# Linear attention joined to wide attention, key sums in column halves, fp32 output projection

## The reference

```python
x = x + _L1_attn_ref(_layernorm(x), W_K, W_Q, W_V, W_O)      # wide attention: 16 heads of 128
x = x + _L1_xattn_ref(_layernorm(x), ctx, ctx, mask, ...)    # linear attention
x = x + _L1_ffn_ref(_layernorm(x), ...)                      # mix of 32 experts
...
# _L1_xattn_ref, 16 heads of 16, 64 features a head
q, k, v = heads(query, Wq, bq), heads(key, Wk, bk), heads(value, Wv, bv)
q_prime = relu(einsum('bhnd,fd->bhnf', q, Wqf))
k_prime = relu(einsum('bhnd,fd->bhnf', k, Wkf)) * attention_mask[:, None, :, None]
kv    = einsum('bhnf,bhne->bhfe', k_prime, v)
qkv   = einsum('bhmf,bhfe->bhme', q_prime, kv)
k_sum = sum(k_prime, axis=2)
qk_sum = einsum('bhmf,bhf->bhm', q_prime, k_sum)[..., None]
out = qkv / (qk_sum + 1e-08)
return out.transpose(0, 2, 1, 3).reshape(B, Sq, H) @ Wo.T + bo
```

## Time and profile before

| | us |
|---|---|
| median of 3 runs | 1010.68 |
| lowest, highest | 1008.80, 1012.94 |
| the profiled execution | 1011.92 |
| its span, first to last instruction | 1010.10 |

### The profile page before, as it was taken

The page is one execution under the profiler, slowest core; times in us unless marked ns, Lnnn a source line. Parts: engine busy times, 40 slices in busy tenths (PEclk is TensorE's granted clock), DMA queues, the critical chain, the costliest instruction groups (busy, mean ns, idle before and its releaser), DMA issues. The chain is left out here.

```text
span 1010.1 us, 19622 instructions
## 1 busy us (share of the span) xinstructions
PE 959.6 (95%) x7403; PEld 820.1 (81%) x7403; DVE 636.9 (63%) x1399; ACT 482.0 (48%) x1611; POOL 239.3 (24%) x257
## 2 busy tenths in 40 slices
PE   7999999999999999999999999999999888999877
PEld 5777777898788888888888888888888757777757
DVE  5678887897765666544554645464554555777854
ACT  3887877334455454353434534444444343344421
POOL 3455786760011111111111111111111130110000
PEclk9999999999999999999999999999999997899979
DMA  8000000003400000000000000000000070000002
GB/s 303 27 2 2 2 2 1 2 15 133 177 14 1 1 1 1 2 1 1 1 1 1 1 1 16 28 1 1 1 2 1 1 268 1 2 1 2 2 1 84
DMA packets 10395, 27.85 MB, mean 28 GB/s; under 512 B 1792, under 2 KB 6944, under 8 KB 9664
## 3 DMA queue, kind: packets, MB, share of 16 engines
q1 hardware_dynamic: 9584, 26.41, 7.2%
q10 hardware_dynamic: 720, 0.20, 0.1%
HBM read 24.51 MB, written 2.10 MB: 26 GB/s over the span
## 5 line engine op out<-in xcount | busy, mean ns | idle before, releaser
L938 POOL TENSOR_TENSOR wa_prob<-wa_prob,wa_rsum 128x512 f32<-128x512 f32 x64 | 67.5, 1055 | 412.5 <-DVE wa_rsum L1493 412.5
L1296 ACT ACTIVATE wa_prob<-wa_prob,wa_negmax 128x128 f32<-128x128 f32 x256 | 99.8, 391 | 56.8 <-DVE wa_negmax L1482 56.6
L41 PE MATMUL bank<-norm_xT_hi,wide_hi 128*128 128x512 f32 x256 | 106.0, 414 | 0.2 <-DVE norm_xT_lo L175 0.2
L42 PE MATMUL bank<-norm_xT_lo,wide_hi 128*128 128x512 f32 x256 | 101.0, 395 | 0.0
L43 PE MATMUL bank<-norm_xT_hi,wide_lo 128*128 128x512 f32 x256 | 101.0, 395 | 0.0
L1549 DVE TENSOR_TENSOR wa_z_lo<-bank,wa_z_hi 128x512 fp32r<-128x512 f32 x64 | 44.3, 691 | 86.6 <-ACT wa_z_hi L1330 86.2
L562 ACT ACTIVATE v_prob<-bank,la_negmax 128x128 f32<-128x128 f32 x256 | 91.1, 399 | 1.1 <-DVE la_negmax L640 1.1
L1304 ACT COPY wa_q<-bank 128x512 f32<-128x512 f32 x64 | 37.5, 586 | 99.0 <-PE bank L43 99.0
L1311 ACT COPY wa_v<-bank 128x512 f32<-128x512 f32 x64 | 37.3, 585 | 97.1 <-PE bank L43 97.1
L308 POOL TENSOR_TENSOR v_prob<-v_prob,la_rsum 128x512 f32<-128x512 f32 x64 | 66.5, 1041 | 52.5 <-DVE la_rsum L645 52.4
L41 PE MATMUL bank<-wide_hi,wa_z_hi 128*128 128x256 f32 x256 | 73.6, 287 | 1.7 <-DVE wa_z_lo L1549 1.4
(11 more groups left out here) (282 smaller groups left out, 2462.8 us busy)
## 6 DMA issues: line engine op xcount, KB each, us to landing
wide_raw<-in_wide_w SPq DMA_DIRECT2D x16, 512.0 KB, 6.4
em_w<-in_em_w SPq DMA_DIRECT2D x1, 4096.0 KB, 16.1
x<-in_x SPq DMA_DIRECT2D x4, 512.0 KB, 4.8
lc_kt<-in_ctx_rev SPq DMA_DIRECT2D x1, 2048.0 KB, 10.6
lc_toep<-in_toeplitz SPq DMA_DIRECT2D x1, 2048.0 KB, 14.5
out_x<-x SPq DMA_DIRECT2D x8, 256.0 KB, 2.9
li_kt<-in_ctx_rev SPq DMA_DIRECT2D x1, 1536.0 KB, 8.2
w_or_y<-in_l_w SPq DMA_DIRECT2D x1, 1024.0 KB, 6.5
```

Of the source, the lines that this page charges most:

```text
L41: nc.tensor.matmul(out, a[0], b[0], start=start, stop=False, skip_group_check=True)
L42: nc.tensor.matmul(out, a[0], b[1], start=False, stop=False, skip_group_check=True)
L938: nc.gpsimd.tensor_tensor(prob[:, s], prob[:, s], rsum[:, s, :].unsqueeze(2).to_broadcast([P, G, P]), ALU.mult).then_inc(prob_ok, 1)
L1296: last = nc.scalar.activation(prob[:, s, j, :], prob[:, s, j, :], ACT.Exp, bias=negmax[:, s, j:j + 1], scale=SCALE, accum_out=sums[:, s, j ...
```

## The change

- The barrier, the release of semaphores and the warm-up multiply are gone. Both stages become one, `stage_both_layers`: each engine goes on from the last head of wide attention into linear attention. Semaphores whose counts have ended are used again from the count that they reached (`Event`, `reached`).
- Buffers of linear attention lie over weights of wide attention that are no longer read (`layer.close()`). SyncE loads the constants before group 3, ctx in four pieces after head 4 of the last group, and the mix's weights after head 16.
- In the last group's heads, ACT, DVE and GpSimd get early work: the split of all of ctx in heads 6 to 9, the split of the weights Q, K, V in heads 10 to 12, norm statistics of images 4 to 7 in head 7 and their apply in head 14, three clears in head 10. TensorE runs the queries of images 0 to 3 behind the weighing of head 14, and the keys around that of head 15. The relu of the second query features is shared out between ACT (two banks) and DVE (two banks), in four banks of their own.
- Key sums: each head has its own matmul, 64 columns of weights and 32 moving columns, with results in partitions 0 to 63 and 64 to 127 (L1017), 16 matmuls in place of 8.
- The output projection is two plain fp32 matmuls of `o` and the unsplit weights (L1041) in place of six fp32r ones; the split of o is gone, `o` has two buffers.
- `vector_setup` moves from image 3 to image 1, the scaling in it (L2244) becomes `vector_length` in image 5, and the transposes of `em_simT` move from the tail into image 14. The wide weights' casts wait for all four pieces of a quarter.

```diff
--- stage_both_layers (was stage_attention_conv_experts_and_wide_attention)
+        layer.close()
+        mix = ExpertMix(pr)
+        linear = linear_attention(pr, lambda n, shape, dt=F32: ctx.enter_context(nc.sbuf_tensor(n, shape, dt)), mix)
+        mix.allocate(ctx)
...
+            linear.sync(sp)
+            mix.sync_stores(sp)
...
+                    if last and t == H - 1:
+                        linear.tensor_keys(pe, 0)
                     weigh(it, t)
+                    if last:
+                        linear.tensor_early(pe, t)
+                        norm.enter_stage(2, 1, b_p)
+                    if last and t == H - 1:
+                        linear.tensor_keys(pe, 1)
...
+            linear.tensor(pe)
+            mix.tensor_program(pe)
...
--- linear_attention
+    FIRST_BANKS = (banks[0], banks[1], banks[6], banks[7])
+    KT_AT, W_AT = 6, 10
+    QUERIES_AT, KEYS_AT = 14, 15
+    STATS_AT, CLEAR_AT, APPLY_AT = 7, 10, 14
     MIX_AT = {0: 3 * G, 1: 3 * G + 1, 2: 3 * G + 3}
+    SIM_AT = 3 * G + 2
+    SETUP_AT, LENGTH_AT = 1, 5
...
-        sp.dma_start(kt32[:, :, 0:G], io["ctx_rev"][:, :, 0:G]).then_inc(kt_first, 16)
+        sp.wait_ge(pr.wide_u_ps, 2 * (NG - 1))
         for t, src in ((bqk[:], io["li_bqk"]), (wf[:], io["li_wf"]), (mask[:], io["li_mask"]),
                        (v_bias[:], io["li_v_bias"]), (out_bias[:], io["li_o_bias"])):
-            sp.dma_start(t, src).then_inc(loaded, 16)
-        sp.wait_ge(kt_first, 16)
-        sp.dma_start(kt32[:, :, G:NB], io["ctx_rev"][:, :, G:NB]).then_inc(kt_loaded, 16)
+            sp.dma_start(t, src).then_inc(loaded.sem, 16)
+        heads_done(sp, 4)
+        for t in range(NG):
+            own = slice(t * G, (t + 1) * G)
+            sp.dma_start(kt32[:, :, own], io["ctx_rev"][:, :, own]).then_inc(kt_in.sem, 16)
+        heads_done(sp, H)
         mix.sync_loads(sp)
-        sp.dma_start(mix.w[:], io["em_w"]).then_inc(mix.w_loaded, 16)
+        sp.dma_start(mix.w[:], io["em_w"]).then_inc(mix.w_loaded.sem, 16)
...
+    def tensor_early(pe, t):
+        if t == QUERIES_AT:
+            norm.enter_stage(4, 2, [b_p] * 2)
+            pe.wait_ge(norm.s_lo, DC * norm.split(0))
+            reached(pe, w_lo, 3)
+            for m in range(DC):
+                queries(pe, 0, m, banks[m])
+
+    def tensor_keys(pe, m):
+        reached(pe, qT_ok, m + 1)
+        keys(pe, 0, m, banks[m])
...
         def key_values(n):
-            pe.wait_ge(kf_ok, n + 1)
-            pe.wait_ge(v_ok, n + 1)
+            reached(pe, kf_ok, n + 1)
+            reached(pe, v_ok, n + 1)
             wait(pe, kv_ok, n)
             wait(pe, x_ok, n - 1)
             for t in range(T):
-                last = nc.tensor.matmul(b_kv[:, t * 2 * VW:(t + 1) * 2 * VW], kp[:, n % 2, t, :],
-                                        va[:, n % 2, 2 * t:2 * t + 2, :], start=True, stop=True)
-            last.then_inc(kv_ps, 1)
+                for e in range(2):
+                    last = nc.tensor.matmul(b_kv[F * e:F * e + F, t * VW:(t + 1) * VW],
+                                            kp[:, n % 2, t, F * e:F * e + F], va[:, n % 2, 2 * t + e, :],
+                                            start=True, stop=True)
+            last.then_inc(kv_ps.sem, 1)
...
         def project(n):
-            pe.wait_ge(ot_lo, n + 1)
-            pe.wait_ge(kv_ok, min(n + 2, NB))
+            reached(pe, o_ok, n + 1)
+            reached(pe, kv_ok, min(n + 2, NB))
             wait(pe, x_ok, n)
             for c in range(DC):
-                last = product(nc, b_kv[:, 0:D], pair(oT, slice(None), n % 2, c), pair(w, slice(None), O, c),
-                               c == 0, c == DC - 1)
-            last.then_inc(o_ps, 1)
+                last = nc.tensor.matmul(b_kv[:, 0:D], o[:, n % 2, c, :], w32[:, O, c, :], start=(c == 0),
+                                        stop=(c == DC - 1))
+            last.then_inc(o_ps.sem, 1)
...
-        pe.wait_ge(pr.w_loaded, 16)
-        warm = w32.rearrange("p w c n -> p (w c n)")
-        for m in range(3):
-            nc.tensor.matmul(b_f[:, m, :], warm[:, m * P:(m + 1) * P], warm[:, 0:512], start=True, stop=True)
-        pe.wait_ge(w_lo, 1)
-        queries(0, 0, b_p)
-        queries(0, 1, b_nd)
-        pe.wait_ge(loaded, 16 * NLOAD)
+        reached(pe, loaded, 16 * NLOAD)
         query_features(0, 0)
-        pe.wait_ge(w_lo, 2)
-        keys(0, 0, b_p)
-        pe.wait_ge(qT_ok, DC)
-        keys(0, 1, b_nd)
-        pe.wait_ge(w_lo, 4)
+        first_query_features()
+        key_features(0)
+        reached(pe, qf_first, 1)
         values(0)
-        key_features(0)
+        turn_x(1, 0)
+        reached(pe, qf_ok, DC)
+        reached(pe, clear, 3)
+        key_values(0)
         values(1)
-        query_features(0, 1)
-        key_values(0)
...
+    def scalar_early(act, t):
+        if KT_AT <= t < KT_AT + NG:
+            own = slice((t - KT_AT) * G, (t - KT_AT + 1) * G)
+            reached(act, kt_in, 16 * NG)
+            nc.scalar.copy(kt[0][:, :, own], kt32[:, :, own]).then_inc(kt_hi.sem, 1)
+        if W_AT <= t < W_AT + 3:
+            n = (Q, K, V)[t - W_AT]
+            act.wait_ge(pr.w_loaded, 16)
+            heads_done(act, 8)
+            nc.scalar.copy(w[0][:, n], w32[:, n]).then_inc(w_hi.sem, 1)
+        if t == QUERIES_AT:
+            reached(act, loaded, 16 * NLOAD)
+            for m in range(DC):
+                keep_qT(act, 0, m, banks[m])
+        if t == KEYS_AT:
+            for m in range(DC):
+                keep_kT(act, 0, m, banks[m])
...
-        def keep_o(n):
-            act.wait_ge(o_ok, n + 1)
-            wait(act, o_ps, n - 1)
-            nc.scalar.copy(oT[0][:, n % 2], o[:]).then_inc(ot_hi, 1)
...
-        def o_rest(n):
-            dve.wait_ge(ot_hi, n + 1)
-            nc.vector.tensor_tensor(oT[1][:, n % 2], o[:], oT[0][:, n % 2].bitcast(F32), ALU.subtract)\
-                .then_inc(ot_lo, 1)
...
-            if n == 3:
+            if n == SETUP_AT:
                 mix.vector_setup(dve)
+            if n == LENGTH_AT:
+                mix.vector_length(dve)
```

More of the change, by code:

```diff
@@ L1 @@
+from collections import namedtuple
 from contextlib import ExitStack
@@ L21, with reached, __init__ @@
 BASE = 2
+Event = namedtuple("Event", "sem base")
+def reached(eng, event, count):
+    eng.wait_ge(event.sem, event.base + count)
 class Chain:
-    def __init__(self, eng, sem, it, per):
-        self.eng, self.sem, self.it, self.per, self.n = eng, sem, it, per, 0
+    def __init__(self, eng, sem, it, per, base=0):
+        self.eng, self.sem, self.it, self.per, self.n, self.base = eng, sem, it, per, 0, base
     def done(self, ins):
@@ L32, in done @@
         ins.then_inc(self.sem, 1)
-        self.eng.wait_ge(self.sem, self.it * self.per + self.n)
+        self.eng.wait_ge(self.sem, self.base + self.it * self.per + self.n)
     def close(self):
@@ L53, in __init__, with event @@
         self.sems = []
+        self.finished = []
+    def event(self, name):
+        return self.finished.pop(0) if self.finished else Event(self.sem(name), 0)
     def sem(self, name):
@@ L795, in stage_attention_conv_experts_and_wide_attention, with stage_both_layers @@
+def stage_both_layers(pr, layer, lora):
     nc, io, x, banks = pr.nc, pr.io, pr.x, pr.banks
@@ L966, in _ @@
                 group(it, it == NG - 1)
+            linear.gpsimd(pool)
+            mix.gpsimd_finish(pool)
         @block.tensor
@@ L1332, in group @@
                         high_part(FRONT_PIECES + t - 1)
+                    if last:
+                        linear.scalar_early(act, t)
                     for unit in late:
@@ L1385, in _ @@
                 group(it, it == NG - 1)
+            linear.scalar(act)
+            mix.scalar_program(act)
         @block.vector
@@ L1556, in group @@
                         low_part(FRONT_PIECES + t - 1)
+                    if last:
+                        linear.vector_early(dve, t)
                     if t == H - 1 and not last:
@@ L1628, in _, with both_layers @@
                 group(it, it == NG - 1)
-def first_layer_and_wide_attention(pr):
+            linear.vector(dve)
+            mix.vector_program(dve)
+def both_layers(pr):
     nc = pr.nc
@@ L2480, in stage_linear_attention_and_expert_mix @@
[L2480 to L2510 removed]
+        stage_both_layers(pr, ctx, lora)
```

1448 lines of the change are left out of this document (727 added, 721 removed).

## The result

The changed kernel takes 977.14 us (median of 4 runs, 976.68 to 977.83), the kernel before beside it 1011.71 (4 runs); the ratio is 0.9663 with a 95% interval of 0.9639 to 0.9686. Forecast were 978, and 967 to 993. The profiled execution took 976.68 us with a span of 974.90.

A forecast was written before the change was run, and what follows sets the result against it. TensorE was taken as the bound, busy 959.6 of 1010.1 us. Stretches A to H summed to 33.0 less, from the profiled 1011.92 to 978.9; 1.2 less for the median gave 977.7, so 978, range 967 to 993.

The forecast's parts named there:

- A: Junction up to nd(0), the start of numerators_and_denominators(0): 9.8 us less, nd(0) at 820.2 against 830.06.
- B: Stretch nd(0) to nd(1), image 0 to image 1: 13.00 to 5.1 us, 7.9 less.
- C: Stretch nd(1) to nd(2): 10.28 to 7.8 us, 2.5 less, half of it the clock.
- D: Stretch nd(2) to nd(4): 1.0 us less (0.5 to 1.5).
- E: Stretch nd(4) to nd(6): 21.01 to 15.0 us, 6.0 less, with L2244 no longer ahead of image 3's key features.
- The term for each image: Each image of the loop: 0.8 us less of TensorE, key sums 0.9 less and the fp32 projection 0.1 more.
- F: Stretch nd(6) to nd(12), 45.65 us before: 6 x 0.8 less 0.3, 4.5 us less.
- G: Stretch nd(12) to nd(15): 1.2 us less, as DVE sets the pace and loses three oT_lo of 0.42.
- H: From nd(15) on: 0.1 us less, split of o (0.9) gone, two fp32 projections 0.4 more each at the lower clock.
- Rival 4: Tail from nd(15) on: the clock stays up there, 970 us; chance 8%.
- Rival 1: Key sums: half-wide records run one after the other without overlap, no gain, costing 14: 992 us; chance 12%.
- Rivals 2, 3 and 5: Lower clock comes back, 986, 15%; narrow key-sum records cost as much as wide, 1021, 3%; early work doesn't hide, 993, 2%.

The follow-up runs named there:

- The late first work: Changed kernel with queries and keys of images 0 to 3 behind the last wide projection instead of in heads 14 and 15: 981.89 us.

## Why the prediction held, point by point

**A was right in size and in its reason.** nd(0) at 820.10 against 820.2, TensorE's wide work ending at 811.4 against 811.3, the wait for the x update 0.53 against 0.4. The late first work confirms 3.1 us of it. As said above, part of the agreement to 0.1 is luck, since single traces differ by up to 2 us before these heads. **The cover in the heads was not complete.** I costed the early work at 0, with head 7 at 6.9 of 7.84 us busy on DVE. But a busy share under 1 does not say that the order fits. The cast, the statistics and then the usual work of the changed kernel, behind each other on DVE, and the wait on TensorE:

```profile
752.33 1.22 DVE L1225 TENSOR_TENSOR li_kt_lo<-li_kt,li_kt_hi 128x1024 fp32r<-128x1024 f32 x1 [0.26 <-ACT li_kt_hi L1143]
753.48 1.40 DVE L126 BATCH_NORM_STATS2 norm_stats<-x 128x6 f32<-128x256 f32 x4
...
757.53 0.68 DVE L2461 COPY wa_probT<-bank 128x512 f32<-128x512 f32 x1
...
758.27 1.16 PE L2035 MATMUL bank<-wa_probT,wa_v 128*128 128x128 f32 x8 [0.60 <-DVE wa_probT L2461]
```

wa_probT comes late and weighing waits 0.60; the head lasts 8.60 instead of 7.85, the next 7.95. With the casts in the loop the same heads last 7.84 and 7.85. So the casts in the heads bring 0.6 in image 0 and cost 0.85 here.

**B was right in size, with the wrong share for the casts.** I named the chain and the casts together. The chunk of x before the loop is what matters: 5.5 of it (4.6 and 0.9). The casts alone are 0.6. The split of o, which the prediction held to be off the path in the middle of the loop, is worth 1.0 at its start: with it back nd(0) to nd(1) takes 6.45. **C and D** followed.

**E was right in size, and half wrong in its reason.** "In image 3 a 2.88 us DVE operation stands ahead of the key features" was true, but its move is worth 1.0 alone. With the casts and the split of o gone it is not needed for more, and with the split of o alone gone the wait falls from 1.79 to 1.34. The key sums in halves give 1.3 of the 5.84 (nd(4) to nd(6) takes 16.50 with the wide ones). The clock adds to the waits: outside the tail those of 1.34, 1.42, 1.44 and 1.45 us, and one of 1.65 at 243 us in every trace, left it up; those of 1.79, 1.99, 2.13, 2.14, 2.99 and 3.76 were followed by the lower level.

**The term for each image was too large**: 0.8 forecast, 0.49 measured (F). Three sizes make it up. Key sums gave 0.77 of the 0.9 (0.90 from first to last record, but the last takes 0.15 until the next step begins). The projection cost 0.15, the upper end of its bounds, where 0.1 was taken. And the step from the values to the key sums takes 0.10 more, which the sum put at nothing: 0.77 less 0.15 less 0.10 is 0.52. **The Trainium skill**'s rule that a change of tiling mode drains the engine (TensorEngine Tiling (Array Packing), Key Properties) names this step, and the traces agree: 0.11 becomes 0.21 behind the values, and where four transposes stand between, 0.43 becomes 0.53 and 0.49 becomes 0.59. Over 16 images that is 1.6 us, the lower end of the 1.6 to 3.2 that I worked out and then left out of the sum. The other rule that I weighed (Instruction Overhead), 60 cycles a matmul, would put 32 records at 0.8 us; they start within 0.90, so it is not contradicted here, and in the numerators, 32 in 1.01, neither.

**G** gave 0.8 more than expected: DVE was not the only limit there, and the key sums' gain came through (with wide ones nd(12) to nd(15) takes 18.48, 1.4 more).

**H failed**: 0.1 forecast, 3.7 measured. Rival 4 ("the clock stays up in the tail") had it, at 8%, and happened in part. Its gain made good what F lacked, and that is luck, since the same program from nd(15) on takes up to 3.5 us more in another trace. Without H, 31.5 were measured against 32.9; with it, against 33.0 stand 35.2 in the profile and 34.6 in the medians.

**The rivals.** Rival 1, no overlap, would have been 986 (the run with the halves in turn) and not 992; the price per image was 0.7 and not 0.9. Rivals 2, 3 and 5 did not come, except for the 0.85 us in the heads.
